# Attention on one core: the softmax denominators of a query block in four matmul groups of 128 columns

## What is computed

```python
q = (x @ Wq.T).reshape(N, S, H, hd).transpose(0, 2, 1, 3)   # k, v likewise
energy = jnp.einsum('nhqd,nhkd->nhqk', q, k)
attn = jax.nn.softmax(energy / jnp.sqrt(jnp.float32(hd)), axis=3)
out = jnp.einsum('nhql,nhld->nhqd', attn, v)
...
x = _layernorm(x + _L0_attn_ref(x, Wq, Wk, Wv), axis=-1)
x = _layernorm(x + _L0_ffn_ref(x, weights, scale, bias), axis=-1)
```

## Time and profile before

| | us |
|---|---|
| median of 3 runs | 2921.0 |
| lowest, highest | 2919.51, 2922.0 |
| span of the profiled execution | 2917.2 |
| of it before the attention's first score | 608 |
| attention, first score to last denominator | 2023 |
| behind it | 286 |
| PE, PEld, DVE, ACT, POOL busy | 2785.6, 1423.5, 2319.8, 2300.0, 343.1 |

### The profile page before, as it was taken

One profiled execution on the slowest core, in us unless ns is written; L12 is line 12 of the kernel. 1 busy time (PEld: TensorE's weight loads), 2 busy tenths in 40 slices (PEclk: granted clock), 3 DMA queues, 4 the chain that ended last, 5 costly groups with the idle time before them and its releaser, 6 DMA issues.

```text
span 2917.2 us, 79173 instructions
## 1 busy us (share of the span) xinstructions
PE 2785.6 (95%) x29276; PEld 1423.5 (49%) x29276; DVE 2319.8 (80%) x2050; ACT 2300.0 (79%) x2789; POOL 343.1 (12%) x342
## 2 busy tenths in 40 slices
PE   8999999979999999999999999999999999997998
PEld 7888888833333333333333333344343333335887
DVE  4334343469898898989889899898989989897998
ACT  3333333379999999999999999999999999894665
POOL 0000000010000000000000000000000000004665
PEclk9999999989999999999999999999999999998999
DMA  5544445556675766767576675767667576655553
GB/s 190 182 179 173 173 173 180 182 134 144 143 160 117 166 130 140 154 138 153 119 168 128 141 164 123 160 121 162 137 142 167 117 161 134 132 122 182 187 206 130
DMA packets 223563, 445.69 MB, mean 153 GB/s; under 512 B 15442, under 2 KB 130130, under 8 KB 198868
## 3 DMA queue, kind: packets, MB, share of 16 engines
q0 software_dynamic: 27504, 200.29, 35.6%
q1 hardware_dynamic: 186596, 224.71, 24.7%
q10 hardware_dynamic: 9216, 16.78, 1.5%
HBM read 123.47 MB, written 117.96 MB: 83 GB/s over the span
## 4 chain that ended last, share of the span: by engine, by line
PE 73%; issue 4%; ACT 2%; DVE 1%; POOL 0%; ACTq 0%; DMA 0%; SPq 0%; DVEq 0%; POOLq 0%
PE banks L637 33%; PE banks L666 30%; PE banks L1008 6%; PE banks L683 2%; ACT probs L764 1%; PE banks L997 1%; PE banks L990 1%; PE banks L1004 1%; ACT L764 0%; POOL score_rows L587 0%; PE banks L991 0%; DVE partial L821 0%; ACT y L1026 0%; DVE stats L1071 0%; DVE score_rows L773 0%
## 5 line engine op out<-in xcount | busy, mean ns | idle before, releaser
L764 ACT ACTIVATE probs<-banks 128x1024 f32<-128x1024 f32 x2048 | 1891.9, 1149 | 99.6 <-PE banks L637 95.3
L637 PE MATMUL banks<-score_rows 97*32 97x512 f16 x16384 | 1186.8, 384 | 90.1 <-issue 65.8
L666 PE MATMUL banks<-probs,v_keys 128*32 128x512 f32 x8192 | 1094.5, 598 | 3.4 <-issue 3.1
L637 PEld LDWEIGHTS banks<-score_rows 97*32 97x32 f16 x16384 | 431.6, 95 | 1076.1 <-ACT probs L764 578.0
L821 DVE TENSOR_TENSOR partial<-partial,probs 128x2048 f32<-128x2048 f32 x384 | 879.7, 2291 | 50.0 <-ACT probs L764 37.7
L818 DVE TENSOR_TENSOR partial<-probs 128x2048 f32<-128x2048 f32 x192 | 440.2, 2293 | 78.6 <-ACT probs L764 74.0
L606 POOL DMA_DIRECT2D total<-partial x191 | 164.9, 863 | 1847.8 <-DVE partial L821 865.5
L666 PEld LDWEIGHTS banks<-probs,v_keys 128*32 128x32 f32 x8192 | 287.3, 112 | 181.3 <-issue 9.5
L821 DVE TENSOR_TENSOR total<-total,probs 128x2048 f32<-128x2048 f32 x128 | 292.7, 2287 | 2.6
L348 DVE TENSOR_TENSOR qk_lo<-banks,qk_hi 128x512 f16<-128x512 f32 x128 | 88.5, 692 | 240.8 <-ACT qk_hi L292 240.8
L292 ACT ACTIVATE qk_hi<-banks 128x512 f16<-128x512 f32 x128 | 76.4, 597 | 234.2 <-PE banks L246 234.2
(11 more groups left out here) (94 smaller groups left out, 2164.1 us busy)
## 6 DMA issues: line engine op xcount, KB each, us to landing
total<-partial POOLq DMA_DIRECT2D x191, 1024.0 KB, 8.2
x_in<-in_L_attn_x SPq DMA_DIRECT2D x17, 1024.0 KB, 7.3
scratch_q_raw<-qk_raw SPq DMA_DIRECT2D x16, 1024.0 KB, 5.5
scratch_k_raw<-qk_raw SPq DMA_DIRECT2D x16, 1024.0 KB, 5.6
scratch_v<-v_out SPq DMA_DIRECT2D x16, 1024.0 KB, 5.0
score_rows<-scratch_q_hi SPq DMA_DIRECT2D x128, 128.0 KB, 6.4
score_rows<-scratch_k_hi SPq DMA_DIRECT2D x128, 128.0 KB, 3.8
v_keys<-scratch_v SPq DMA_DIRECT2D x64, 256.0 KB, 6.9
```

The lines of the kernel that those rows point to most:

```text
L637: last = nc.tensor.matmul(scores_of(unit)[part, i, :], k_rows[:, h, keys], q_rows[:, h, qb * BLK:(qb + 1) * BLK], start=True, stop=True)
L666: last = nc.tensor.matmul(banks[rows, out_bank(qb), :], v_keys[:, kt, rows], probs[:, kt % P_RING, h, :], start=(kt == 0), stop=(kt == KT ...
L764: nc.scalar.activation(probs[:, kt % P_RING, heads, :], scores_of(qb * UNITS + u), ACT.Exp, scale=SCALE / GAIN ** 2).then_inc(a_prob, 1)
```

## The change

The group of 512 columns becomes four groups of 128, behind key tiles 9, 10, 11 and 12. The first waits for merges and copy as the old one did; each adds one to `a_den`, and the counts that DVE waits for are multiplied by four. The loop of TensorE now starts at tile 13, and the denominators of an item's last block are made inside the steps of the next item's first block.

```diff
-DEN_TILE = 10
+DEN_TILES = (9, 10, 11, 12)
...
-    HEAD = DEN_TILE + 1
+    HEAD = DEN_TILES[-1] + 1
...
-        pe.sem_inc(a_den, 2)
+        pe.sem_inc(a_den, 2 * len(DEN_TILES))
...
-        def denominators(it, qb):
+        def denominators(it, qb, piece):
             st = it * QB + qb
...
+            width = BLK // len(DEN_TILES)
+            cols = slice(piece * width, (piece + 1) * width)
+            split = it is LAST and qb == QB - 1
+            parts = [total[:, qb % 2], partial[:, GROUPS - 2]] if split else [total[:, qb % 2]]
+            if piece == 0:
+                if split:
+                    pe.wait_ge(a_merged, (st + 2) * (GROUPS - 1) - 1)
+                    pe.wait_ge(a_sum, (st + 1) * KT + P_RING)
+                else:
+                    pe.wait_ge(a_merged, (st + 2) * (GROUPS - 1))
+                pe.wait_ge(a_out, st + 1)
             for part in parts:
                 for h in range(G):
                     rows = slice(HD * h, HD * h + HD)
-                    last = nc.tensor.matmul(banks[rows, out_bank(qb), :], ones[:], part[:, h, :],
+                    last = nc.tensor.matmul(banks[rows, out_bank(qb), cols], ones[:], part[:, h, cols],
                                             start=(part is parts[0]), stop=(part is parts[-1]))
             last.then_inc(a_den, 1)
...
-                if kt == DEN_TILE and qb > 0:
-                    denominators(it, qb - 1)
+                if kt in DEN_TILES and qb > 0:
+                    denominators(it, qb - 1, DEN_TILES.index(kt))
+                elif kt in DEN_TILES and not (isinstance(it, int) and it == 0):
+                    denominators(it - 1, QB - 1, DEN_TILES.index(kt))
...
-            denominators(it, QB - 1)
+            else:
+                for piece in range(len(DEN_TILES)):
+                    denominators(it, QB - 1, piece)
...
-            dve.wait_ge(a_den, st + 1 + 2)
+            dve.wait_ge(a_den, (st + 1 + 2) * len(DEN_TILES))
...
-                            dve.wait_ge(a_den, st + 1)
+                            dve.wait_ge(a_den, (st + 1) * len(DEN_TILES))
```

## The result

The changed kernel takes 2991.5 us (median of 4 runs, 2979.4 to 3004.9) against 2921.5 (2919.5 to 2922.5): a ratio of 1.0247, interval 1.0211 to 1.0283. It is slower by 70 us. The profiled execution has a span of 2981.4 us, 64 above that of the earlier trace rows.

What follows compares the result with a forecast made beforehand. ScalarE sets the pace, losing 9.1 us a round. Denominators 0.4, top 1.5, block 1 4.2, block 3 4.3 and the rest 2.0 make 12.4; 15 times 3.3 is 49, so 2921 + 49 = 2970 us, range 2900 to 3010.

Steps and rivals of the forecast that it cites:

- (1) The lump goes: Denominators: a piece takes 0.22 us, 0.05 to 0.1 exposed in place of 0.36; gain 0.27 a block, 1.1 a round.
- R3: Rival, chance 0.05: pieces cost more than a quarter; at 0.29 us the gain is gone, at 0.87 the total is 3117.
- (2) Waits: Merge and copy waits moved with the pieces cost nothing here: at least 1.9 us of room, and 1.7 for the copy.
- (3) The top of the loop: Loop's top moves from tile 11 to 13; its code packet fits between merges: 1.5 us in place of 4.3, gain 2.8.
- longest not at the top: Sign: TensorE's "issue" waits under 2 us at the top, near 3 us each at tile 12/13 of blocks 1 and 3.
- R4: Rival, chance 0.06: the top's request is late and meets the next merge; 5 to 7 us more a round, 3050.
- (4) Block 1, tile 12: Code packet waits behind the block's first merge, late by 2.9 to 3.4 us; costs ScalarE 4.2 a round instead of 0.
- (4) Block 3: Existing 1.20 us stall behind a merge grows to 2.5 to 3.4; costs ScalarE 4.3 a round in place of 1.35.
- Half clock: Two stretches of TensorE half clock a round, behind the stalls of blocks 1 and 3, and neither at the top.
- R5: Rival, chance 0.07: no difference, gains and new stalls cancel.
- R1: Rival, chance 0.14: code comes in time, boundaries miss the merges; 2843 to 2862, or 2905 if the top's gain fails too.
- R2: Rival, chance 0.12: only one of the block 1 and block 3 collisions happens; round loses 8.2 or 8.1, 2907.

Runs made afterwards that it cites:

- pair of kernels with small merges: Merges cut to 4 of 2048 numbers a row: the kernel before, 2833.5 us, and the changed kernel with 60 unexecuted instructions added, 2808.7 us.
- four_shift96 with small merges: Changed kernel with 96 unexecuted instructions added ahead of the loop and merges of only 4 of 2048 numbers a row: 2862.5 us.
- four_shift60: Changed kernel with 60 unexecuted instructions added, last code boundary 221 ahead of the loop's end (161 in the changed kernel): 2889.5 us.
- its pair with small merges: Changed kernel with 60 unexecuted instructions added and merges of only 4 of 2048 numbers a row: 2808.7 us.
- four_head14_shift20: Changed kernel with TensorE's loop starting at tile 14 and 20 unexecuted instructions added, last boundary 229 ahead of the end: 2861.4 us.
- one_small_merges: Kernel before (one group of 512 columns) with merges of only 4 of 2048 numbers a row: 2833.5 us.
- four_head11: Changed kernel's four pieces, but TensorE's loop starts at tile 11 as before, first block's pieces made of zeros: 2955.6 us.
- four_shift96: Changed kernel with 96 unexecuted instructions added ahead of the loop, last boundary 1 instruction ahead of its end: 2995.1 us.

## Why the prediction was right in its direction, and which steps of it failed

Forecast 2970, range 2900 to 3010, measured 2991.5. The direction, the cause in the large (packets with code, held by merges) and the size within a third (+49, measured +70) held. That the size did is luck, as the sum below shows. The steps:

- **What bounds the kernel.** Right: ScalarE's busy time is the same and its wait for scores carries the whole difference.
- **(1) The lump goes.** Right. A piece takes 0.22 us, and 0.06 us a block is exposed, the forecast's 0.05 to 0.1. That is 1.25 us a round less, and the pair of kernels with small merges shows about as much. R3 falls with it: at 0.22 us for eight records, a record takes 27 ns. The Trainium skill ("TensorE: Matmul & The Clock Gate", Back-to-back issue gap) has some 81 ns for a load and matmul of 128 columns; with four column groups side by side the trace shows a third of that.
- **(2) Waits.** Right: 3.5 us in the whole execution.
- **(3) The top of the loop.** Wrong, and the largest miss: "1.5 us in place of 4.3", measured 7.15 against a mean of 3.6. The failed step is "The packet fits between". It reckoned with one packet, asked for at the branch. There are two. (Its price for a request that meets nothing, 1.9 us, starts from a trigger 80 instructions past a boundary, which no row shows. In four_shift96 with small merges, where I take the request to go out at the branch, the packet starts 0.9 to 1.5 us behind it.) The first holds the loop's top, is asked for by position (161 instructions from the last boundary to the end, 210 before), met the old merge's data and started at the branch:

```profile
q0 software_dynamic: 132, 0.97, 94.3%
```

```profile
q8 instruction: 1, 0.02, 5.0%
```

These are the only queues with more than stray packets in 1411.4 to 1416.5 and, for q8, in 1416.5 to 1417.6. TensorE went on 2.4 us later and only then ran into the trigger of the second packet, and that met the next merge (issued at 1417.66, 1.2 us behind the branch and not 2.5). With small merges, where nothing is in the way, the top of the four pieces still loses 2.7 us a round; the other 4.5 come with the merges' data. The sign "longest not at the top" failed with this step. So R4 was half the truth, at a chance of 0.06 and with another cause. The Trainium skill ("Runtime: NRT & Kernel Launch", Instruction fetch mechanics) warns that a taken branch whose target is outside the two pages at hand needs a fetch of the target first. I had used that section's "mostly hidden" and passed over this rule; the runs agree with it, with the addition that here the fetch starts ahead of the branch where position and merges allow.

- **(4) Block 1, tile 12.** Wrong: 4.2 forecast, 0.1 measured. The failed step is "fills the DMA engines from 1418.2 to 1423.4 [...]. Usable 1425.7", that a packet waits for the end of the data. The prediction's reading behind it, that no q8 packet starts while a merge moves data, does not hold for the trace of the kernel before either: in 31 of its 190 merges one starts at least 0.5 us ahead of the end of the data, the earliest 3.2 us in. In the changed kernel it is 74 of 190. The merge in question in the changed kernel, issued at 1446.80, in 1448.2 to 1455.0:

```profile
q0 software_dynamic: 144, 1.05, 76.9%
q8 instruction: 1, 0.02, 0.9%
```

The packet started at 1450.14, 1.9 us behind the first data. It was usable at some 1452.5, and TensorE came to the boundary at 1452.8. In each of the 14 rounds the packet at this place started 1.9 to 2.6 us behind the first data.
- **(4) Block 3.** Right: 1228 matmuls behind the top, a gap of 2.64 where 2.5 to 3.4 were forecast, 3.6 us lost against 4.3.
- **Half clock.** Forecast twice a round, behind the stalls of block 1 and block 3, and not at the top. Block 1 had no stall, and the top has it in 13 of 14 rounds. Block 3 has it in 7 of 15 (granted clock below 0.75 over the 3.2 us behind the stall). The windows of the changed kernel behind the stall of 4.01 and behind that of 2.64 (length; busy times; granted clock, DMA share, GB/s):

```profile
1425.20:1428.40 3.20, 3.20 (x28) 1.44 (x32) 0.00 (x0) 1.82 (x2) 0.86 (x1) 0.61 0.27 65
1515.50:1519.00 3.50, 3.49 (x52) 1.35 (x52) 1.93 (x2) 2.41 (x3) 0.86 (x1) 1.00 0.60 120
```

A round earlier block 3's stall, 3.47 us up to 1384.27, was followed by 0.61 over 3.2 us. The length of the stall alone does not decide it: stalls in block 3 of 2.64 and 2.65 us are followed by 1.00 in three rounds and by 0.56 or 0.57 in two. As means, the top's two stalls of 1.2 and 3.5 us cost ScalarE 7.15, block 3's of 2.7 costs it 3.6.
- **The sum.** 12.4 a round forecast, 13.4 measured, on a base of 8.7 and not 9.1. It came out near since the 4.2 put on block 1 is about the 5.6 that was missing at the top. Two large errors offset each other; the total alone would not have shown them.

R5 and R1 fall by the result. Of R2 the condition came true, block 1's collision was missed, and its time (2907) did not, since R2 kept the forecast's 1.5 for the top. That a better alignment leads below the kernel before, as R1 and R2 had it, is shown by 2889 and 2861.

What stays open: how many instructions behind a boundary the request goes out exactly, and which packet has to wait for the end of a merge's data and which slips in between. A placement can be ranked from this, but its time was forecast badly more often than well. Of the twelve kernels' times five fell into the range expected (four_shift60, its pair with small merges, four_head14_shift20, one_small_merges, and four_head11 by its total only) and seven did not.

## What to carry to other kernels

When the code of a loop's body is fetched anew in each round, as here with 14 to 16 packets, the order and number of instructions have a second cost beside the one in the trace's rows: where the 256-instruction boundaries stand against the DMA traffic. A change of a few us a round can be buried under it or faked by it, so compare such changes at more than one alignment, moved by unexecuted instructions, before keeping or dropping them; here the same four pieces are 2.5% slower or 2.0% faster than the one group as it stood. Look at "issue" stalls behind each branch and count the instructions from the last boundary to the branch: with 1 or 18 the top's packet was late in every run, with 210 to 229 it was late only where a merge stood in its way. With 161 or 162 it started 0.4 us ahead at best in the four kernels shown, and with 2.4 us from its start to usable code that is too late.

## What the hardware showed that was not expected

- **Instructions that are never executed changed the time by 106 us.** four_shift96 and four_shift60 differ by 36 of them: 2995.1 and 2889.5.
- **The packet with a loop's top is fetched in every round**, at a time set by position. Without merges' data it starts 2.9 us ahead of the branch with 221 instructions from the last boundary, 2.1 with 210, 0.3 with 161, and 1.0 behind it with 1 (medians of 14 rounds). With 221, in 1345.5 to 1346.5, branch at 1348.76:

```profile
q8 instruction: 1, 0.02, 7.2%
```

- **A packet with code does not always wait for the end of a merge.** In the changed kernel it can start 0.2 us into the data, 1.9 as above, or only at their end, and the merge takes longer too: the same 144 packets that fill 99.8% of 5.2 us in the earlier trace rows take 6.8 us with one code packet among them. Of the changed kernel's merges without SyncE's transfers beside them the 60 with no code packet among them take 5.2 to 6.4 us, median 5.5, and the 20 with one 6.4 to 6.9, median 6.7.
- **The end of the loop has a price of its own.** In four_shift60 the last item, whose code stands behind the loop, makes ScalarE idle once for 9.46 us, behind a stall of TensorE by "issue" of 7.77. It is not so everywhere: in four_shift96 the same place is cheap, and that round loses 3.5 us where the others lose 14.4. Why is not shown. The idle time in four_shift60:

```profile
2502.42 1.94 ACT L773 ACTIVATE probs<-banks 128x1024 f32<-128x1024 f32 x2 [9.46 <-PE banks L637]
```
